# Second attention: where the weighing of the values stands in TensorE's order, in steps with the first half of a pair's sums

## The reference, cut to what matters

```python
q, k, v = _fq_sym(q, axis=-1), _fq_sym(k, axis=-1), _fq_sym(v, axis=2)
attn = jnp.einsum('bhqd,bhkd->bhqk', q, k)
attn = jax.nn.softmax(attn.astype(jnp.float32), axis=-1)
attn = _fq_unsigned(attn, axis=-1)      # s = max(row)/255; round(attn / s), 0..255, times s
out = jnp.einsum('bhqk,bhkd->bhqd', attn, v)
```

## Time and profile before

| engine | busy us | share of the span |
|---|---|---|
| TensorE, matmul | 1023.4 | 80% |
| TensorE, weight load | 675.3 | 53% |
| VectorE | 860.7 | 67% |
| ScalarE | 688.5 | 54% |
| GpSimd | 510.9 | 40% |

### The profile page before, as it was taken

One profiled execution on the slowest core, in us unless ns is written; L12 is line 12 of the kernel. 1 busy time (PEld: TensorE's weight loads), 2 busy tenths in 40 slices (PEclk: granted clock), 3 DMA queues, 4 the chain that ended last, 5 costly groups with the idle time before them and its releaser, 6 DMA issues. The chain is left out here.

```text
span 1283.1 us, 24452 instructions
## 1 busy us (share of the span) xinstructions
PE 1023.4 (80%) x8536; PEld 675.3 (53%) x8536; DVE 860.7 (67%) x1329; ACT 688.5 (54%) x1137; POOL 510.9 (40%) x580
## 2 busy tenths in 40 slices
PE   1699972589999998457546999999999994479993
PEld 1455542578999997346431333333333333468992
DVE  6322218437888873879898888888888824537874
ACT  1266641114777761117422888888888883114760
POOL 3266643230000004122004887887877873240004
PEclk9899996599999998778865999999999998589997
DMA  3566665033777862010000000000000001043983
GB/s 133 165 179 164 164 174 198 24 121 90 228 224 222 227 184 66 26 40 17 0 1 1 2 2 2 2 2 2 1 2 2 2 2 50 1 156 102 273 247 98
DMA packets 82013, 115.24 MB, mean 90 GB/s; under 512 B 9488, under 2 KB 52112, under 8 KB 81552
## 3 DMA queue, kind: packets, MB, share of 16 engines
q1 hardware_dynamic: 78144, 104.78, 27.9%
q0 software_dynamic: 3072, 8.39, 2.0%
q10 hardware_dynamic: 720, 1.06, 0.2%
HBM read 87.98 MB, written 26.21 MB: 89 GB/s over the span
## 5 line engine op out<-in xcount | busy, mean ns | idle before, releaser
L1719 ACT ACTIVATE exps_a<-score,k_scale 128x512 f32<-128x512 f32 x512 | 314.1, 688 | 47.2 <-PE score L1577 42.7
L1734 DVE TENSOR_REDUCE most_a<-look 128x2 f32<-128x1024 f32 x256 | 304.6, 1222 | 43.3 <-PE look L1540 37.6
L1699 POOL TENSOR_SCALAR rounded_a<-exps_a 128x1024 f16<-128x1024 f32 x172 | 180.1, 1047 | 51.5 <-ACT exps_a L1719 41.8
L1589 PE MATMUL out<-exps_a,sum_col_a 128*32 128x256 f32 x2048 | 161.3, 392 | 9.3 <-ACT exps_a L1719 2.8
L1577 PE MATMUL score<-q_now_a,ki_stack 64*128 64x512 bf16 x512 | 159.2, 386 | 5.5 <-ACT exps_a L1719 5.5
L1540 PE MATMUL look<-k_stack,q_stack 64*128 64x512 bf16 x512 | 147.6, 403 | 12.5 <-DVE most_a L1734 9.6
L978 POOL DMA_INDIRECT xn_f<-expert_rows_out,place_f x16 | 15.8, 984 | 319.5 <-DMA expert_rows_out<-rows_out_f 315.3
L1131 DVE TENSOR_TENSOR weights_lo_f<-weights_raw_f,weights_hi_f 128x768 fp32r<-128x768 f32 x113 | 108.2, 958 | 0.1
L522 POOL TENSOR_SCALAR probs<-probs,exp_max_now,exp_min 128x1024 f32<-128x1024 f32 x64 | 78.7, 1237 | 65.2 <-ACT probs L650 65.0
L1589 PEld LDWEIGHTS out<-exps_a,sum_col_a 128*32 128x32 f32 x2048 | 42.0, 108 | 106.1 <-ACT exps_a L1719 80.3
L1699 POOL TENSOR_SCALAR rows<-exps_a 128x1024 f16<-128x1024 f32 x84 | 88.0, 1047 | 22.3 <-ACT exps_a L1719 17.7
(11 more groups left out here) (323 smaller groups left out, 2511.4 us busy)
## 6 DMA issues: line engine op xcount, KB each, us to landing
weights_raw_f<-in_gu_f SPq DMA_DIRECT2D x125, 256.0 KB
weights_raw_f<-in_d_f SPq DMA_DIRECT2D x125, 128.0 KB
keys<-flat_k_halves SPq DMA_DIRECT2D x40, 256.0 KB, 4.9
rows_in_f<-expert_rows_in SPq DMA_DIRECT2D x34, 256.0 KB, 3.3
expert_rows_out<-rows_out_f SPq DMA_DIRECT2D x32, 256.0 KB, 3.2
flat_k_halves<-flat_k SPq DMA_DIRECT2D x20, 256.0 KB, 2.5
queries<-flat_q_halves SPq DMA_DIRECT2D x80, 64.0 KB, 2.5
expert_rows_in<-blank_o SPq DMA_DIRECT2D x1, 4608.0 KB, 14.9
```

Of the source, the lines that this page charges most:

```text
L1589: last = pe.matmul(out[rows, part * 256:(part + 1) * 256], sum_col[:, :], exps[(first + i) % EXPS][:, h, part * 256:(part + 1) * 256], sta ...
L1699: pool.tensor_scalar(rounded[step % ROUNDED][:, :, :], exps[step % EXPS][:, :, :], 1.0, -SHIFT if step // 2 % 2 else SHIFT, ALU.mult, ALU. ...
L1719: act.activation(exps[step % EXPS][:, h, :], score[(2 * step + h) % SCORES][:, :], ACT.Exp, scale=sh.k_scale[:, c, 2 * (group % PAIRS) + h ...
L1734: dve.tensor_reduce(most[n // UNITS % 2][:, n % UNITS // KT, :, n % KT], look[bank_of["look", n]][:, :, :], AX.X, ALU.max).then_inc(look_r ...
```

## The change

In the loop of TensorE the two lines that issue an even step's weigh move from behind the sums to in front of them. Nothing is added or taken out; no other engine's code is touched; the weigh at c = 1 keeps its place behind the sums.

```diff
                     if step < STEPS:
                         scores(step, 1)
+                    if c % 2 == 0 and c != 2 and 4 <= step <= STEPS:
+                        weigh(step - 4)
                     if 2 <= step < STEPS + 2 and (c not in (2, 3) or group in (0, GROUPS)):
                         sums((step - 2) // 2 * 2, (step - 2) % 2)
                     elif c == 3 and step < STEPS:
...
                         sums(step - 3, 1)
                     if c == 1 and group:
                         weigh(step - 3)
-                    if c % 2 == 0 and c != 2 and 4 <= step <= STEPS:
-                        weigh(step - 4)
                     if c == TURN_AT and group + 1 < GROUPS:
                         turn_queries(group + 1)
```

## The result

The changed kernel took a median of 1273.62 us over 22 runs (1266.37 to 1280.52), the kernel before 1276.14 us over as many. The ratio is **0.9967**, with a 95% interval of 0.9953 to 0.9982: 4.2 us faster (2.3 to 6.0), where 3.8 were forecast. (The two medians alone lie 2.5 apart; the gain is read from the ratio, whose interval holds both.) It is a small gain that is clear of noise. The profiled execution has a span of 1272.4 us. The stage itself, from its first score to its last fold, takes 374.0 us in the trace before and 368.5 in the trace after.

What follows compares the result with a forecast made beforehand. The stage was taken as a ring of waits, with GpSimd without slack from rounding 9 to the last weigh. Gains 0.7 + 14 x 0.17 = 2.4 + 0.7 make 3.8 us; 1275.04 - 3.8 = 1271 us, range 1264 to 1278.

Steps and rivals of the forecast that it cites:

- The price of an even step: TensorE, steps awaiting an exponential: score to weigh 0.31, weigh to sums 0.21, sums to score 0.57; 0.17 us gained.
- No pause between weigh and sums: TensorE, weigh then sums, both in form 128*32: no added drain, 0.21 us between their starts.
- slower rival: Weigh then sums pauses TensorE 0.12 us more per step; ring grows 0.19 per group, 1277.3 us in all; chance 0.13.
- Most of the local gain is absorbed: Of 0.75 us gained locally per group, most becomes a longer TensorE wait at c = 1; total gain 3.8 us.
- Where it is absorbed: GpSimd has no slack from rounding 9 to the last weigh, 10.23 us; gains of c = 10, 12, 14, 0 end at c = 1.
- Sums to turn: TensorE at c = 14: the turn was taken to start 0.57 us after the sums, a distance not shown before.
- The 0.07 of c = 0: At c = 0 only some 0.07 us is waited and gained; its weigh may wait 0.2 to 0.3 for rounding 13.
- Only c = 6 reaches the period: Only c = 6's 0.17 us shortens the ring, period 23.14 to 22.97; c = 4 and 8 gain nothing.
- unmoved rival: Nothing moves: c = 7's looks wait for VectorE's bank, or another wait replaces c = 6's; 1274 us; chance 0.15.
- The sum: Whole stage: group 0 gains 0.7 us, groups 1 to 14 2.4, the last group 0.7; together 3.8.
- The sign in the waits: TensorE's wait for GpSimd at L1604 grows from about 3 us to some 6 to 10, 0.3 to 0.6 per group.
- The gain stays whole: GpSimd absorbs nothing: 14 x 0.75 + 6 x 0.17 + 0.75 = 12.3 us gained, 1262.8 us; chance 0.12.

Runs made afterwards that it cites:

- four weighs: Against the kernel before, only the weighs of c = 0, 10, 12 and 14 moved ahead of the sums: usual group 23.06 us against 23.07, ratio 0.9998.
- lengthening the chain: The change plus one useless GpSimd instruction behind rounding 12 of groups 1 to 15: usual group 23.25 us against 22.81, ratio to before 1.0053.
- With scale_heads moved: The change plus GpSimd's scale_heads moved from behind rounding 10 to behind rounding 7: usual group 22.61 us, ratio to before 0.9937.
- c = 6 alone: Against the kernel before, only the weigh of c = 6 moved ahead of the sums: usual group 22.85 us against 23.07, ratio 0.9957.
- the two moves on GpSimd: scale_heads behind rounding 7, two of six shift instructions behind rounding 10: with the change ratio to before 0.9907, median 1268.06 us; without it 0.9975.

## Why the prediction was right, point by point

- **The price of an even step.** Predicted 0.31, 0.21 and 0.57 with a gain of 0.17, the lower reading; measured 0.30, 0.23 and 0.54, a gain of 0.20 to 0.21 at c = 6, 10 and 12. What the low reading missed is mainly the last term: the sums leave for the next form 0.03 earlier when a weigh has stood ahead of them.
- **No pause between weigh and sums.** Right: 0.23. The slower rival needed 0.06 more per step, and none came.
- **Most of the local gain is absorbed.** Right, and shown from three sides: by position (0.01 from four weighs), by lengthening the chain (0.44 for an instruction of 0.40) and by shortening it (0.20 and 0.37 more).
- **Where it is absorbed.** Mostly right, in two places wrong. "Sums to turn is not shown; I take 0.57" failed: the turn of c = 14 waits for the shift setting, 0.75 behind the sums, so c = 14 keeps its 1.83 us from score to score and its gain ends there and not at c = 1. With scale_heads moved, when the shifts are set earlier, the turn follows the sums by 0.56 and c = 14 takes 1.64. The 0.07 of c = 0 does not reach c = 1 either: its weigh waits for rounding 13, as the prediction had feared, by 0.10 and not by 0.2 to 0.3, since c = 14 brought nothing, and c = 0 keeps its 1.40. The chain is the same, so the sum did not change. The count behind the chain was off by one: the 0.05 stands at 13 of the 15 group ends before, and two are late.
- **Only c = 6 reaches the period.** Nearly: c = 6 alone gives 0.22 and the whole change 0.26. c = 8 was called neutral and got shorter by 0.08, of which c = 7 gave 0.05 back: its looks now wait for VectorE's bank, the tie that the unmoved rival named, and this wait shortens the one at c = 8. c = 4 gave 0.02.
- **The sum.** Too small in its main term. By the two traces group 0 gave 0.5 us where 0.7 was forecast, groups 1 to 14 gave 4.5 where 2.4 was, and the last group with the end of the stage 0.6 where 0.7 was: 5.5 together instead of 3.8. In the main term 14 x 0.17 = 2.4 should have been 14 x 0.26 = 3.6. Of the three long groups of before, two lost their 0.2 us: the delay fell into TensorE's new wait; two short groups (1 and 3) gave 0.2 more each. In group 0 of the changed kernel's trace c = 4 is 0.36 longer than before instead of 0.17 shorter, because more of it lies in the slow clock (last section). That 4.2 by the ratio comes so near to 3.8 is in part luck, within an interval of 2.3 to 6.0. The 1271 is also counted from a median of three runs, 1275.04, where 22 runs gave 1276.14.
- **The sign in the waits.** The forecast of 6 to 10 us for TensorE's wait at L1604 was wrong as a reading of the list, which shows 38.7; in the timeline the added wait at c = 1 is 0.4 per group, 6 us in all, as forecast.
- **The rivals.** "The gain stays whole" (22.3 per group) is refuted by 22.81. "Nothing moves" (1.4 us or less) is refuted by the interval, which begins at 2.3, and by the 0.22 per group of c = 6.

## What to carry to other kernels

Work that is moved into an engine's wait pays only where no other engine's chain ends at the same consumer. Before pricing such a move, follow that consumer's other inputs back to the first point where they have slack: here a start 0.05 us behind its releaser in group after group marked the bound, although that engine had the lowest busy share of the four in this stage (GpSimd: 18.53 of 23 us, and 40% of the whole span). And when a gain is absorbed, look for idle gaps upstream of the absorbing chain, or inside it, and shift work of the chain into them: the two moves on GpSimd together with the change were worth three times the change, and without it 0.10 us per group.

## What the runs showed of the hardware that was not expected

- Where another form follows the sums (eight f32 matmul records of 256 columns, form 128*32), it starts 0.57 after their first start. It starts 0.53 or 0.54 after it where four f16 matmuls of the weigh stood just ahead: in groups 1 to 14 of the changed kernel's trace at 81 of 84 places (turns aside); at the other three the sums had waited and it is 0.57. Why is not shown.
- The four extra matmuls of the weigh at c = 10, whose form the profile gives as 128*16, cost no pause next to those in 128*32: the sums start 0.44 after the weigh, 0.21 for four more matmuls on top of the 0.23.
- TensorE's clock rises once, in c = 4 of group 0, after the stage has begun at the lower of its two levels (0.50 of full speed, 1.2 GHz). In the kernel before c = 4 begins at 701.90, and the full clock comes about 1 us later; in the changed kernel it begins at 698.52, and the full clock comes 1.8 us later. The place of the weigh does not decide this: among the six kernels that move it at c = 4, that step takes from 1.53 to 2.17 us in group 0, and 1.77 to 2.16 among the five that don't. By stretches, TensorE's clock in the third column from the end, before and then after:

```profile
702.00:703.00 1.00, 1.00 (x8) 0.17 (x11) 0.25 (x2) 0.38 (x1) 0.95 (x1) 0.52 0.00 0
703.00:704.00 1.00, 1.00 (x16) 0.27 (x14) 1.00 (x1) 0.89 (x2) 0.03 (x1) 1.00 0.00 0
```
```profile
699.00:700.00 1.00, 1.00 (x12) 0.28 (x12) 0.41 (x1) 0.76 (x2) 0.57 (x1) 0.50 0.00 0
700.00:701.00 1.00, 1.00 (x16) 0.18 (x8) 0.81 (x1) 0.51 (x1) 0.41 (x1) 0.83 0.00 0
```

- The three long groups of before have their delay at c = 12 of group 2, c = 14 of group 7 and c = 0 of group 13. In the step ahead of each, an exponential starts 0.78 to 0.80 after its score instead of 0.51. The first is there in all eleven traces. The other two are there in the five kernels in which the weighs of c = 10 to 0 stand behind the sums; in the others the group is as long as its neighbours. What delays the exponentials was not tried.
